# Graph layer on one core: result stores moved from GpSimd's queue to SyncE's, first pair additions and first index columns placed earlier

## What is computed

```
h    = relu(layernorm(x))                      # per node row
agg[type, dst] += h[src] * norm                # per edge, segment sum
node = sum over types of agg[type] @ (w_comp @ weight)[type]
out  = x + relu(node + bias + h @ loop_weight)
```

## Time and profile before

| | us |
|---|---|
| median of three runs | 1066.85 |
| the profiled execution's own time | 1066.05 |
| its span, first to last instruction | 1064.3 |
| PE busy | 1043.9 (98%) |
| DVE busy | 1018.1 (96%) |
| ACT busy | 925.4 (87%) |
| POOL busy | 805.2 (76%) |

### The profile page before, as it was taken

One profiled execution on the slowest core, in us unless ns is written; L12 is line 12 of the kernel. 1 busy time (PEld: TensorE's weight loads), 2 busy tenths in 40 slices (PEclk: granted clock), 3 DMA queues, 4 the chain that ended last, 5 costly groups with the idle time before them and its releaser, 6 DMA issues. The chain is left out here.

```text
span 1064.3 us, 23588 instructions
## 1 busy us (share of the span) xinstructions
PE 1043.9 (98%) x4903; PEld 664.6 (62%) x4903; DVE 1018.1 (96%) x4370; ACT 925.4 (87%) x3252; POOL 805.2 (76%) x1381
## 2 busy tenths in 40 slices
PE   5999999999999999999999999999999999999997
PEld 2444444444444444444444444444899999999997
DVE  6999999999999999999999999999999999999995
ACT  6999999999999999999999999999588888888884
POOL 7888888888888888888888888886555555555553
PEclk9999999999999999999999999999999999999999
DMA  4323232323232444222232323222599999999993
GB/s 105 94 77 83 76 101 69 93 66 103 66 94 73 125 116 134 77 81 83 76 88 72 93 76 85 75 66 80 173 300 298 297 297 299 295 295 301 296 299 96
DMA packets 91092, 150.97 MB, mean 142 GB/s; under 512 B 18578, under 2 KB 57826, under 8 KB 90946
## 3 DMA queue, kind: packets, MB, share of 16 engines
q0 software_dynamic: 28224, 76.93, 26.0%
q1 hardware_dynamic: 61250, 71.78, 22.0%
q10 hardware_dynamic: 1472, 0.74, 0.3%
HBM read 97.88 MB, written 51.49 MB: 140 GB/s over the span
## 5 line engine op out<-in xcount | busy, mean ns | idle before, releaser
L463 POOL DMA_INDIRECT xg<-x,idx x392 | 389.8, 994 | 75.3 <-issue 49.0
L704 PE MATMUL y_ps<-w_all,hT 128*128 128x512 f32 x784 | 401.7, 594 | 0.7 <-issue 0.7
L710 PE MATMUL y_ps<-w_all,hT 128*128 128x512 f32 x784 | 400.5, 592 | 0.0
L559 ACT ACTIVATE z<-y_ps,mix 128x128 f32<-128x128 f32 x784 | 245.0, 364 | 56.9 <-PE y_ps L710 37.2
L710 PEld LDWEIGHTS y_ps<-w_all,hT 128*128 128x128 f32 x784 | 148.9, 190 | 188.4 <-issue 182.7
L892 DVE SCALAR_TENSOR_TENSOR sum_b<-y_ps,mix,sum_b 128x128 f32<-128x128 f32 x784 | 265.3, 338 | 0.0
L704 PEld LDWEIGHTS y_ps<-w_all,hT 128*128 128x128 f32 x784 | 141.3, 191 | 141.1 <-issue 122.4
L416 POOL TENSOR_TENSOR u<-z 128x128 f32<-128x128 f32 x392 | 181.8, 464 | 36.4 <-ACT z L559 28.1
L512 POOL DMA_DIRECT2D out<-res x98 | 76.1, 777 | 133.0 <-DVE res L1131 133.0
L587 ACT ACTIVATE hw<-xw,shift,nrstd 128x128 f32<-128x128 f32 x392 | 162.7, 482 | 1.7
L777 PE MATMUL y_ps<-w_loop,hwT 128*128 128x128 f32 x782 | 151.1, 274 | 0.0
(11 more groups left out here) (95 smaller groups left out, 1406.2 us busy)
## 6 DMA issues: line engine op xcount, KB each, us to landing
seg<-msgs SPq DMA_DIRECT2D x391, 96.8 KB
msgs<-msg SPq DMA_DIRECT2D x98, 258.0 KB
xw<-x POOLq DMA_DIRECT2D x97, 256.0 KB, 5.1
out<-res POOLq DMA_DIRECT2D x97, 256.0 KB, 4.3
type_bc<-type_rows SPq DMA_DIRECT2D x56, 112.0 KB
xg<-x,idx POOLq DMA_INDIRECT x392
w_all<-weight ACTq DMA_DIRECT2D x1, 512.0 KB
dst_i<-dst ACTq DMA_DIRECT2D x1, 196.0 KB, 3.3
```

The costliest lines, as they stand in the source:

```text
L463: nc.gpsimd.indirect_dma_start(xg[:, q, j, :], None, x, bass.IndirectOffsetOnAxis(ap=idx[:, q, j:j + 1], axis=0)).then_inc(s_gather[q * G ...
L559: ins = nc.scalar.activation(z[:, r, b, :], y_ps[r][:, b, :], ACT.Copy, scale=mix[:, q, j, b:b + 1])
L704: nc.tensor.matmul(y_ps[r][:, B // 2:B, :], hT[:, q, j, :], w_all[:, B // 2:B, :], start=True, stop=True).then_inc(s_y_high, 1)
L710: nc.tensor.matmul(y_ps[r][:, 0:B // 2, :], hT[:, q, j, :], w_all[:, 0:B // 2, :], start=True, stop=True).then_inc(s_y, 1)
```

## The change

`store_results` goes from GpSimd's program to SP's. On SP it stands at the head of `reload_windows(g)`, ahead of the table read and the four segment loads, and what is left after the last group is stored by SP, which then waits for all stores. GpSimd's `load_x` keeps the bare wait on `n_res` that the store had. The pair addition of tile 0 goes ahead of the fourth gather of group 2, those of tiles 1 to 3 behind the first three gathers of group 3. The load of the index array is cut in two: columns 0 to 7 (groups 0 and 1) with a semaphore of their own, and the rest, for which GpSimd waits at group 2.

```diff
-            sp.dma_start(src_all[:, :], src).then_inc(s_src, 16)
+            sp.dma_start(src_all[:, 0:FIRST], src[:, 0:FIRST]).then_inc(s_src_first, 16)
+            sp.dma_start(src_all[:, FIRST:NT], src[:, FIRST:NT]).then_inc(s_src, 16)
...
+            def store_results(g, q, full=G, last=0):      # on sp
+                r = q % NRING
+                sp.wait_ge(n_res, g + 1)
+                if full:
+                    sp.dma_start(OUT_WIN[:, bass.ds(g * G, full), :], res[:, r, 0:full, :]).then_inc(n_out[r], 16)
+                if last:
+                    sp.dma_start(out[(NW - 1) * P:N, :], res[0:last, r, full, :]).then_inc(n_out[r], 16)
+
             def reload_windows(g, n, q, full=G, last=0):
-                sp.wait_ge(n_res, g - (LRING - 1))
+                store_results(g - LRING, q)
                 load_windows(g, q, row_tab, n_seg[q], full, last)
...
+            for g in range(NGW - LRING, last_g):
+                store_results(g, g % NRING)
+            store_results(last_g, last_g % NRING, LAST_FULL, LAST)
+            for r in range(NRING):
+                sp.wait_ge(n_out[r], 16 * (len(range(r, NGW, NRING)) + (r == last_g % NRING and LAST_FULL > 0)))
...
-            pool.wait_ge(s_src, 16)
+            pool.wait_ge(s_src_first, 16)
...
+                    if g == FIRST // G:
+                        pool.wait_ge(s_src, 16)
...
+                    if g == 2 and j == G - 1:
+                        add_pair(0, 0)
                     (gather j)
                     if j == 2 and not is_before(g, 3):
                         gains(g - 2, (q - 2) % RING)
-                    if not is_before(g, 3):
+                    if g == 3 and j < G - 1:
+                        add_pair(j + 1, (j + 1) % RING)
+                    if not is_before(g, 4):
                         add_pair(g * G + (j - 3 * G), (q * G + j) % RING)
...
             def load_x(g, n, q, full=G, last=0):          # on pool
-                store_results(g - LRING, q)
+                pool.wait_ge(n_res, g - LRING + 1)
...
-                store_results(g, g % NRING)
-            store_results(last_g, last_g % NRING, LAST_FULL, LAST)
-            for r in range(NRING):
-                pool.wait_ge(n_out[r], ...)
```

More of the change, by code:

```diff
@@ L33 @@
 CHUNKS = 2
+FIRST = 8
 DV = 2
@@ L235, in build_layer @@
         s_step = sem("s_step")
+        s_src_first = sem("s_src_first")
         s_src = sem("s_src")
@@ L395, in _ @@
                     load_windows(q, q, row_tab, c_reload)
+            def store_results(g, q, full=G, last=0):
[5 more added lines that the diff above has]
+                    sp.dma_start(out[(NW - 1) * P:N, :], res[0:last, r, full, :]).then_inc(n_out[r], 16)
             def reload_windows(g, n, q, full=G, last=0):
-                sp.wait_ge(n_res, g - (LRING - 1))
+                store_results(g - LRING, q)
                 load_windows(g, q, row_tab, n_seg[q], full, last)
             sweep(sp, NGW - 1, reload_windows, LRING, LRING, LRING)
-            g = NGW - 1
-            reload_windows(g, g // LRING, g % LRING, LAST_FULL, LAST)
+            last_g = NGW - 1
+            reload_windows(last_g, last_g // LRING, last_g % LRING, LAST_FULL, LAST)
+            for g in range(NGW - LRING, last_g):
[3 more added lines that the diff above has]
+                sp.wait_ge(n_out[r], 16 * (len(range(r, NGW, NRING)) + (r == last_g % NRING and LAST_FULL > 0)))
         @block.gpsimd
@@ L540, in _ @@
                     window_relative(ahead, ahead // LRING, ahead % LRING, G if ahead < last_g else LAST_FULL + 1)
-                store_results(g, g % NRING)
-            store_results(last_g, last_g % NRING, LAST_FULL, LAST)
-            for r in range(NRING):
-                pool.wait_ge(n_out[r], 16 * (len(range(r, NGW, NRING)) + (r == last_g % NRING and LAST_FULL > 0)))
         @block.scalar
```

## The result

| | before | after |
|---|---|---|
| median of six runs on one chip, us | 1066.89 (1066.74 to 1069.30) | 1063.03 (1062.15 to 1063.62) |
| profiled execution, us | 1066.05 | 1063.62 |
| its span, us | 1064.3 | 1061.8 |
| last result written, us | 1058.61 | 1059.21 |
| last result to end of span, us | 5.66 | 2.56 |

The ratio is 0.9957 [0.9944, 0.9970], faster by 3.9 us. Run again later, the same pair gave 0.9966 [0.9952, 0.9979], faster by 3.2. The profiled pair differs by 2.5 us: 3.1 gained behind the last result, 0.6 lost ahead of it. The other 1.4 of the 3.9 us lie in which execution was profiled: the one before took 0.8 us less than its median, the one after 0.6 more than its own.

What follows compares the result with a forecast made beforehand. PE was taken to bound both stages, leaving start, end and DMA engines open. Span 1064.3 - 2.6 (end) + 0 + 0 + 0 = 1061.7; median 1066.85 - 2.6 = 1064.2 us, range for 8 in 10 1062.2 to 1081.

Steps and rivals of the forecast that it cites:

- the likeliest case: Whole kernel: the time comes out as forecast, 1064.2 us, own range 1062.4 to 1065; chance 0.42.
- Part 1, the end: Behind the last result: SP's quicker issue, landing and short DRAIN gain 2.6 us, bounds 0.7 to 3.0.
- The rival by which the DRAIN goes to SP at 2 us: Kernel end: SP's DRAIN is long, or landings slow; gain only 0.7 to 1.1 us, about 1066; chance 0.10.
- Part 2, SP's queue: Node stage: with the store SP's queue takes 2.7 of 3.12 us a group, so it costs nothing.
- Part 3, the DMA engines: Node stage: stores in 512 B packets add 0.27 us a group, share 0.98 to 1.07, hidden by PE, cost nothing.
- the q10 row: ACT's queue of 503 B packets: at its 14.5 B/ns a 256 KB store costs 1.13 us, +0.27 a group.
- The Trainium skill's rule: About 3 cycles a packet beside one per 32 B: single-row stores cost 16% more, +0.14 us a group, share 1.02.
- The rival of the DMA engines as the bound: Node stage: transfers exceed 3.12 us a group, slower than before, most of it 1069 to 1081 us; chance 0.33.
- Part 4, the start: Start, index split and moved additions: between 0.7 us gained and 1.1 us lost, taken as 0.
- The rival by which GpSimd comes out of the start 1.1 us late: Start: the last gather of group 3 costs 1.1 us, giving 1065.3, within the noise; chance 0.15.
- the waits for z of tiles 0 and 3: Start: GpSimd waits before the last gathers of groups 2 and 3; later additions come up to 1.1 us later.
- PE's 0.70 us: Start: PE's longest wait between its first product and the steady stage, before 26.36; about 0.7 us to be had.

Runs made afterwards that it cites:

- pool_waits: The changed kernel, with GpSimd instead of SP waiting at its end for the stores that SP issues: 1064.41 us, 0.9992 of the kernel before.
- split_store: The changed kernel with each full group's store issued by SP in two halves: 1124.11 us, 1.0547 of the kernel before.
- extra2_before: The kernel before with a further, unused load of 128 KB in every group of the node stage: 1071.14 us, 1.0052 of the kernel before.
- extra2_after: The changed kernel with a further, unused load of 128 KB in every group of the node stage: 1070.11 us, 1.0047 of the kernel before.
- adds_only: The kernel before with only the first pair additions moved among the gathers: 1065.52 us, 1.0005 of the kernel before.
- changed_again: The changed kernel unaltered, run again on another chip: 1063.11 us, 0.9966 of the kernel before.
- adds_but_last: The kernel before with the pair additions moved, but tile 3's left behind the last gather of group 3: 1065.55 us, 0.9993 of the kernel before.
- index_only: The kernel before with only the index load split in two: 1065.01 us, 0.9998 of the kernel before.
- stores_only: The changed kernel with its two edits of the start undone, so only the result stores move to SP: 1061.94 us, 0.9970 of the kernel before.
- tail_only: The kernel before, with SP issuing only the last group's two stores and waiting for all stores: 1062.09 us, 0.9972 of the kernel before.
- split_before: The kernel before with each full group's store issued by GpSimd in two halves: 1066.61 us, 1.0002 of the kernel before.
- tail_two: The kernel before, with the last group's stores moved to SP, except the 80-row one, issued by ScalarE: 1062.58 us, 0.9962 of the kernel before.

## Why the prediction was right

Predicted 1064.2 us, measured 1063.0 (1063.1 when run again), inside the likeliest case's own 1062.4 to 1065. That the span came out almost as forecast, 1061.8 for 1061.7, is luck: the end gave 0.5 us more than I said and the start took 0.6 that I had put at nothing. The medians lie 1.2 us apart, since I gave the changed kernel the 0.8 us between the profiled execution and the median before, and its own median lies under its profiled one.

**Part 1, the end, held, and was 0.5 us too small.** 2.6 us were forecast, 3.1 measured. SP's first issue began 0.03 us after the result, where GpSimd took 0.63, and the second 0.44 us after it, where I had 0.49. The landing took 1.6 us where I took 2.0; 1.6 was my lower bound. From there to the end of the span it was 0.5 us where I had 0.63, with a DRAIN of 13 ns instead of 133. 0.44 + 1.6 + 0.5 are the 2.56 us, but for rounding; all three terms were a little high, the landing most. The rival by which the DRAIN goes to SP at 2 us is out in this kernel, and pool_waits shows the 2 us come back when GpSimd is made to wait.

**Part 2, SP's queue, was the step with the thinnest cover, and I named another.** I put 2.7 of 3.12 us on SP and took the rare long issues for lags that 0.4 us a group would refill. The store's issue took 0.42 us, the top of my range, and a group without a long issue takes 2.85. With the long ones SP's queue is taken for 3.08 us in the mean, and 0.04 us a group is left in the node stage (the waits under split_store), a tenth of what I said. Ordinary running is just covered by that: PE has no gap, and GpSimd waits for segments only before its last two `rel`. But 0.5 us more of issue a group cost 61 us (split_store less the changed kernel, 1124.1 - 1063.0, from different series of runs), while 0.13 us more of DMA time a group cost none. So "cost nothing" came true by a margin that I had ten times too large.

**Part 3, the DMA engines: right in sign and in its conclusion, half the size.** Share 0.98 to 1.02, +0.13 us a group, where the q10 row led me to +0.27. The queues' rows say the same: q1's share rose from 22.0% of 16 x 1064.3 to 30.6% of 16 x 1061.8, +1452 us, q0's fell by 1217, so +235 us of engine time, 0.15 us of all sixteen for each of 98 groups. The same bytes cost 1452 / 1217 = 1.2 times as much on q1 as on q0; the q10 row, 1.13 us against 0.86, had said 1.3. The Trainium skill's rule (DMA: Bandwidth & Descriptors, Why small descriptors are slow), by which I had computed +0.14, agrees with both numbers. The rival of the DMA engines as the bound, to which I gave a third, most of it between 1069 and 1081 us, is not what happens. The share passed 1, and GpSimd waited for segments 3.2 us in the whole program, before the `rel` of the last two groups, PE never:

```profile
POOL rel L450 <- DMA seg<-msgs: 3.2, 2, 2.4
```

extra2_before and extra2_after show gaps first with a seventh more bytes, at 334 to 335 GB/s and shares of 1.05 and 1.09; a share of 1 was never the limit. The q10 row was too far off. That its loads ran among many others at the start may be why; it was not tried.

**Part 4, the start: the zero was wrong by about 1 us, and neither edit alone does it.** Two steps failed. The rival by which GpSimd comes out of the start 1.1 us late, to which I gave 0.15, is nearer to what the start did than the zero of my sum.

The first: I said the histogram waits for the destinations anyway, and that earlier gathers only keep ahead. In fact the split moved both up, GpSimd's index copy from 4.31 to 3.44 and ACT's first pass from 6.18 to 5.31; then ACT and DVE stood still until the first gathered rows landed, while GpSimd went on issuing gathers. ACT in the changed kernel (timeline, idle before in brackets):

```profile
5.31 0.62 ACT L663 ACTIVATE signs<-dst_f,limits 128x392 bf16<-128x392 f32 x1 [1.20 <-DVE limits L833]
...
11.39 0.31 ACT L579 ACTIVATE h<-xg 128x128 f32<-128x128 f32 x1 [1.13 <-DMA xg<-x,idx]
```

In the kernel before ACT came to that line at 11.03 without a wait. The rows were asked for 0.87 us earlier and came no earlier that the traces show (DVE's first pass over them starts at 10.87, and at 10.89 before). From 6 to 8 us the 16 DMA engines have a share of 1.13 here, 1.11 before; that the gather queues behind the weights and index columns in them is the likely reason, and I made no experiment on it. PE's first product is at 17.12 (17.01 before), and its transposes ahead of it now wait longer. In the six traces with the split PE is idle 0.41 to 0.60 us before them and the products run at the lower of the clock's two levels (1.2 GHz, a pair of them in 2.07 us; 1.02 us at 2.4 GHz) until 19.1 to 20.6 us; in the eight without, the idle time is 0.28 to 0.39 us and the upper level is there at 16.9 to 19.5. That the two hang together is a reading of fourteen traces, and not shown.

The second: the waits for z of tiles 0 and 3. I priced them at up to 1.1 us lost and 0.7 won, and took the middle. POOL in the changed kernel:

```profile
18.31 0.94 POOL L482 DMA_INDIRECT xg<-x,idx  x1 [0.31 <-issue]
21.57 0.46 POOL L431 TENSOR_TENSOR u<-z 128x128 f32<-128x128 f32 x1 [2.31 <-ACT z L568]
22.17 0.96 POOL L482 DMA_INDIRECT xg<-x,idx  x1
```

GpSimd stands 2.31 us before the last gather of group 2. It is there 0.4 us earlier than in adds_only, by the split, and z comes at least 1.8 us later, since the first products run at the lower level. In adds_only, where they ran at the upper one from the start, that wait is absent:

```profile
18.69 0.94 POOL L465 DMA_INDIRECT xg<-x,idx  x1 [0.30 <-issue]
19.73 0.46 POOL L416 TENSOR_TENSOR u<-z 128x128 f32<-128x128 f32 x1
```

PE's 0.70 us is gone as I said it might be, and its place is taken by small waits for `sum_a` (the waits from 18 to 60 us, us in all, times, longest):

```profile
PEld y_ps L719 <- DVE sum_a L901: 6.0, 12, 1.1
...
PE y_ps L719 <- DVE sum_a L901: 0.5, 2, 0.3
```

How much this costs is read from two products, tile 3's first half and tile 20's:

| traces | tile 3 starts | tile 20 starts | between |
|---|---|---|---|
| both edits: after, split_store, pool_waits, extra2_after, changed_again | 24.00 to 24.73 | 57.03 to 57.76, mean 57.48 | 33.02 to 33.08 |
| new order alone: adds_only | 22.87 | 55.89 | 33.02 |
| new order but for tile 3: adds_but_last | 23.55 | 56.62 | 33.07 |
| split alone: index_only | 24.63 | 56.27 | 31.64 |
| neither: before, stores_only, tail_only, extra2_before, split_before, tail_two | 22.85 to 24.16 | 56.03 to 57.12, mean 56.45 | 32.04 to 33.67 |

With the old order a late start is caught up: index_only has the third latest start and reaches tile 20 among the first. With the new order the way to tile 20 takes 33.0 us whatever the start, so the lateness that comes with the split stays. Both together are 1.0 us later at tile 20 than neither (57.48 - 56.45), 0.61 in the first pair of traces (57.73 - 57.12). The last result moved by the same 0.60, as it must with 1001.48 us between. By timing this is not to be told: changed_again's -3.2 us equals that of stores_only, whose interval alone is 2.3 us wide.

**What stays open.** Why the medians of changed and stores_only agree where the traces say 1 us; what makes SP's long issues, and what sets the length of GpSimd's DRAIN; why the landing of the first gather doesn't follow its issue; and what the new order would do with the split's late start if tile 3's addition were moved back in that kernel, which was not tried.

**A better version.** tail_two and tail_only are at least as fast as the changed kernel (tail_two 1062.58, changed_again 1063.11, same chip, intervals of the ratios overlap), and they leave SP's queue its slack (44.5 and 48.9 us of waits for `res` from 770 to 1037 us, where the changed kernel has 3.7). Nothing measured is in favour of moving the other 97 stores, or of the edits of the start.

## What to carry to other kernels

Ask of the last microseconds which engine waits last: a wait and two short stores moved off GpSimd at the very end were worth 3.1 us, and the other 97 stores nothing. When work is moved to an idle-looking queue, add up what its instructions cost, table reads and the occasional long issue included, and compare the mean with the period: here most groups took 2.85 of 3.12 us, the mean 3.08, and one more issue a group cost 60 us. What is left of a queue is read from its waits in the stage itself. A step that waits for a fresh result shouldn't stand ahead of work that everything behind it needs, unless the result is known to be early also in a slow start.

## What was unexpected of the hardware

- GpSimd's DRAIN at the block's end took 2.03 us in before, 2.60 in extra2_before and 3.17 in split_before, with all stores landed; 2.21 us in after and 1.95 in pool_waits, where GpSimd stores nothing; and 4.10 us in tail_only, from 1056.1, while its last store was still on the way. SP's took 12 to 133 ns.

```profile
L118 POOLq DRAIN  x1: 4095/4095/4095, 1056.1 to 1056.1; - x1
```

- With a seventh more bytes the node stage ran with small gaps at 334 to 335 GB/s, at recorded shares of 1.05 and 1.09; with 298 GB/s at 1.02 it had none.
- Of SP's issues of `seg<-msgs`, most took 0.32 us and some up to 1.5 us (2.3 before).
- SP's table read took 0.30 us behind one store issue and 0.57 behind two.
- Of nearly the same start, traces of different executions reach TensorE's upper clock level at 16.9 to 20.6 us.
